# Perceiver layer: scores of two heads on the two halves of the array, keys out of PSUM in one instruction per engine

## What is computed

```
q = (layernorm(x) @ Wq + bq)   # 16 heads of 64
k = (ctx @ Wk + bk);  v = (ctx @ Wv + bv)
weights = softmax(q k^T / 8);  x = x + (weights v) @ Wo + bo
```

## Time and profile before

| | us |
|---|---|
| median of three runs | 1577.32 |
| span of the profiled execution | 1574.1 |
| TensorE matmul busy | 1500.4 (95%) |
| VectorE busy | 913.4 (58%) |
| ScalarE busy | 600.4 (38%) |

### The profile page before, as it was taken

One profiled execution on the slowest core, in us unless ns is written; L12 is line 12 of the kernel. 1 busy time (PEld: TensorE's weight loads), 2 busy tenths in 40 slices (PEclk: granted clock), 3 DMA queues, 4 the chain that ended last, 5 costly groups with the idle time before them and its releaser, 6 DMA issues. The chain is left out here.

```text
span 1574.1 us, 24321 instructions
## 1 busy us (share of the span) xinstructions
PE 1500.4 (95%) x8628; PEld 1178.7 (75%) x8628; DVE 913.4 (58%) x1868; ACT 600.4 (38%) x1238; POOL 54.4 (3%) x56
## 2 busy tenths in 40 slices
PE   6899999999999999899999999999999989799999
PEld 3587778777777787687778777777777677588777
DVE  4445753674467447734763575457535555576779
ACT  2324631653256226522641364246315524331120
POOL 3000000000000000000000000000000012200002
PEclk9999999999999999999999999999999988989999
DMA  6600100031011002300100032001003140023210
GB/s 234 201 7 28 33 22 8 28 97 52 9 35 41 8 8 62 103 18 2 54 22 7 15 95 74 8 14 41 14 1 88 27 95 27 1 85 104 82 53 27
DMA packets 87056, 75.96 MB, mean 48 GB/s; under 512 B 9120, under 2 KB 66496, under 8 KB 86928
## 3 DMA queue, kind: packets, MB, share of 16 engines
q1 hardware_dynamic: 85600, 70.29, 15.1%
q0 software_dynamic: 1328, 3.99, 0.9%
HBM read 69.01 MB, written 5.24 MB: 47 GB/s over the span
## 5 line engine op out<-in xcount | busy, mean ns | idle before, releaser
L606 PE MATMUL b_ps<-ctxT,wk 128*128 128x512 f32 x1536 | 410.9, 403 | 9.4 <-DVEq L536 4.5
L597 PE MATMUL b_ps<-wv,ctxT 128*128 128x512 f32 x1536 | 368.2, 398 | 3.6 <-DVE ctxT L195 3.6
L597 PEld LDWEIGHTS b_ps<-wv,ctxT 128*128 128x128 f32 x1536 | 286.8, 188 | 75.4 <-issue 10.9
L606 PEld LDWEIGHTS b_ps<-ctxT,wk 128*128 128x128 f32 x1536 | 281.3, 190 | 67.9 <-issue 7.5
L853 DVE TENSOR_SCALAR_CACHE_REDUCE b_prob<-b_ps 128x512 f32<-128x512 f32 x256 | 176.9, 691 | 211.1 <-PE b_ps L618 209.1
L773 ACT ACTIVATE b_kst<-b_ps,b_bkT 64x512 fp32r<-64x512 f32 x256 | 174.7, 682 | 247.4 <-PE b_ps L606 244.2
L801 DVE COPY b_V<-b_ps 128x512 f32<-128x512 f32 x128 | 88.6, 692 | 253.5 <-PE b_ps L597 253.3
L752 ACT COPY b_pT<-b_ps 128x512 f32<-128x512 f32 x128 | 75.2, 588 | 418.2 <-PE b_ps L627 417.5
L867 DVE SCALAR_TENSOR_TENSOR b_kst<-b_ps,b_bkT,b_kst 64x512 fp32r<-64x512 f32 x256 | 191.8, 749 | 18.2 <-ACT b_kst L773 7.8
L764 ACT ACTIVATE b_prob<-b_prob,b_negm 128x512 f32<-128x512 f32 x256 | 183.0, 717 | 1.9
L618 PE MATMUL b_ps<-b_kst,q 128*128 128x512 f32 x512 | 160.9, 395 | 5.3 <-DVE b_prob L853 4.4
(11 more groups left out here) (207 smaller groups left out, 1227.1 us busy)
## 6 DMA issues: line engine op xcount, KB each, us to landing
stage<-in_ctx SPq DMA_DIRECT2D x32, 512.0 KB, 3.8
q<-q_s SPq DMA_DIRECT2D x128, 64.0 KB, 2.4
stage<-in_L_xattn_Wk SPq DMA_DIRECT2D x30, 256.0 KB, 3.1
stage<-in_L_xattn_Wv SPq DMA_DIRECT2D x28, 256.0 KB, 2.8
w_tiles<-in_L_ffn_q_proj SPq DMA_DIRECT2D x16, 256.0 KB, 4.1
w_tiles<-in_L_ffn_k_proj SPq DMA_DIRECT2D x16, 256.0 KB, 3.8
w_tiles<-in_L_ffn_v_proj SPq DMA_DIRECT2D x16, 256.0 KB, 3.8
w_tiles<-in_L_ffn_o_proj SPq DMA_DIRECT2D x16, 256.0 KB, 3.3
```

What stands on the lines that cost most here:

```text
L597: mm = nc.tensor.matmul(ps[:, bank], ctxT[:, a, k, c * P:(c + 1) * P], wv[:, w, k], start=m == 0 and k == 0, stop=m == 2 and k == C - 1)
L606: mm = nc.tensor.matmul(ps[:, KB + t % 2], wk[:, i % 2, w, k], ctxT[:, a, k, s * BANK:(s + 1) * BANK], start=m == 0, stop=m == len(terms) - 1)
```

## The change

- `score` is called once per block. For each of the three terms (q hi with key hi, q lo with key hi, q hi with key lo) it issues two 64-row products, head 0 from partitions 0 to 63 and head 1 from 64 to 127, into the banks `QB` and `QB + 1`: six instructions of 64 rows where four of 128 rows were.
- P is issued whole, all 12 products, and S behind it. There is one key bank, so P of block t waits for the lo parts of block t-1 (before: t-2).
- The keys leave PSUM with one ScalarE and one VectorE instruction of 128 rows each (before: two and two of 64 rows).
- VectorE's score copies read the two banks; both wait for the last of the six products.
- `q` in SBUF is half as large and is loaded with one DMA (before: four).

```diff
-    KB, QB, TB, OB = 0, 2, 3, 5
+    KB, QB, TB, OB = 0, 1, 3, 5
 def load_q(sp, Z, X, q_s, b, i):
-    for half in range(2):
-        for h in range(2):
-            sp.dma_start(X.q[half * Z.HD:(half + 1) * Z.HD, i % 2, h].bitcast(F32),
-                         q_s[:, i, h * Z.HD:(h + 1) * Z.HD, b * P:(b + 1) * P].rearrange("l d t -> d l t")
-                         ).then_inc(X.q_in[i % 2].sem, 16)
+    sp.dma_start(X.q[:, i % 2].bitcast(F32), q_s[:, i, :, b * P:(b + 1) * P].rearrange("l d t -> d l t")
+                 ).then_inc(X.q_in[i % 2].sem, 16)
...
-            def score(b, t, h):
+            def score(b, t):
...
-                reach(pe, klo_done, b, 2 * t + h + 1)
-                reach(pe, qk_out, b, 2 * t + h)
-                for l in range(2):
-                    mm = nc.tensor.matmul(ps[:, QB], q[:, i % 2, h, l], kst[:, t % 2, h], start=l == 0, stop=l == 1)
+                reach(pe, klo_done, b, t + 1)
+                reach(pe, qk_out, b, 2 * t)
+                for m, (l, a) in enumerate(((0, 0), (1, 0), (0, 1))):
+                    for h in range(2):
+                        rows = slice(h * HD, (h + 1) * HD)
+                        mm = nc.tensor.matmul(ps[:, QB + h], q[rows, i % 2, l], kst[rows, t % 2, a], start=m == 0, stop=m == 2)
                 mm.then_inc(qk_psum.sem, 1)
...
-                    reach(pe, klo_done, batch, 2 * (n - 1))
-                    project(n, 0, 6)
+                    reach(pe, klo_done, batch, n)
+                    project(n, 0, 3 * C)
                 if exists(e, more):
-                    score(*own(b, e), 0)
-                if exists(t, more):
-                    project(n, 6, 3 * C)
-                if exists(e, more):
-                    score(*own(b, e), 1)
+                    score(*own(b, e))
...
-                    for h in range(2):
-                        rows = slice(h * HD, (h + 1) * HD)
-                        nc.scalar.activation(kst[rows, m % 2, h], ps[rows, KB + m % 2], ACT.Identity,
-                                             bias=bkT[rows, m // SB:m // SB + 1]).then_inc(khi_done.sem, 1)
+                    nc.scalar.activation(kst[:, m % 2, 0], ps[:, KB], ACT.Identity,
+                                         bias=bkT[:, m // SB:m // SB + 1]).then_inc(khi_done.sem, 1)
...
-                    for h in range(2):
-                        rows, other = slice(h * HD, (h + 1) * HD), slice((1 - h) * HD, (2 - h) * HD)
-                        reach(dve, khi_done, batch, 2 * m + h + 1)
-                        nc.vector.scalar_tensor_tensor(kst[other, m % 2, h], ps[rows, KB + m % 2],
-                                                       bkT[rows, m // SB:m // SB + 1], kst[rows, m % 2, h].bitcast(F32),
-                                                       ALU.add, ALU.subtract).then_inc(klo_done.sem, 1)
+                    reach(dve, khi_done, batch, m + 1)
+                    nc.vector.scalar_tensor_tensor(kst[:, m % 2, 1], ps[:, KB], bkT[:, m // SB:m // SB + 1],
+                                                   kst[:, m % 2, 0].bitcast(F32), ALU.add, ALU.subtract
+                                                   ).then_inc(klo_done.sem, 1)
```

More of the change, by code:

```diff
@@ L142, in __init__ @@
         self.ctxT = sb("ctxT", [P, 2, Z.C, Z.S], F32R)
-        self.q = sb("q", [P, 2, 2, 2, P], F32R)
+        self.q = sb("q", [P, 2, 2, P], F32R)
         self.wo = sb("wo", [P, Z.NP, Z.D])
@@ L150, in __init__ @@
         self.chi_done = count("chi_done", Z.NC, Z.NC)
-        self.q_in = [count(f"q_in{i}", 4 * 16 * Z.NP // 2, 0) for i in range(2)]
+        self.q_in = [count(f"q_in{i}", 16 * Z.NP // 2, 0) for i in range(2)]
         self.stage = Stage(ctx, nc, Z)
@@ L510, in cross_attention @@
         k_psum = sem("k_psum", STEPS)
-        qk_psum = sem("qk_psum", 2 * STEPS)
+        qk_psum = sem("qk_psum", STEPS)
         t_psum = sem("t_psum", NP * ROUNDS)
@@ L514, in cross_attention @@
         r_psum = sem("r_psum", NP)
-        khi_done = sem("khi_done", 2 * STEPS)
+        khi_done = sem("khi_done", STEPS)
         exp_done = sem("exp_done", 2 * STEPS)
         te_done = sem("te_done", NP * ROUNDS // 2)
-        klo_done = sem("klo_done", 2 * STEPS)
+        klo_done = sem("klo_done", STEPS)
         qk_out = sem("qk_out", 2 * STEPS)
@@ L578, in _ @@
                     if i is not None and (more or i < NP):
-                        reach(sp, qk_psum, (b, 0), 2 * SB * (i - 1))
+                        reach(sp, qk_psum, (b, 0), SB * (i - 1))
                         load_q(sp, Z, X, q_s, b + i // NP, i % NP)
@@ L605, in project @@
                     a, w, k = terms[m]
-                    mm = nc.tensor.matmul(ps[:, KB + t % 2], wk[:, i % 2, w, k], ctxT[:, a, k, s * BANK:(s + 1) * BANK],
+                    mm = nc.tensor.matmul(ps[:, KB], wk[:, i % 2, w, k], ctxT[:, a, k, s * BANK:(s + 1) * BANK],
                                           start=m == 0, stop=m == len(terms) - 1)
@@ L609, in project @@
                     mm.then_inc(k_psum.sem, 1)
-            def score(b, t, h):
+            def score(b, t):
                 i = t // SB
-                if t % SB == 0 and h == 0:
-                    reach(pe, X.q_in[i % 2], b, 64 * (i // 2 + 1))
-                reach(pe, klo_done, b, 2 * t + h + 1)
-                reach(pe, qk_out, b, 2 * t + h)
-                for l in range(2):
-                    mm = nc.tensor.matmul(ps[:, QB], q[:, i % 2, h, l], kst[:, t % 2, h], start=l == 0, stop=l == 1)
+                if t % SB == 0:
+                    reach(pe, X.q_in[i % 2], b, 16 * (i // 2 + 1))
+                reach(pe, klo_done, b, t + 1)
[4 more added lines that the diff above has]
+                        mm = nc.tensor.matmul(ps[:, QB + h], q[rows, i % 2, l], kst[rows, t % 2, a], start=m == 0, stop=m == 2)
                 mm.then_inc(qk_psum.sem, 1)
@@ L769, in step @@
                     reach(act, k_psum, batch, m + 1)
-                    reach(act, qk_psum, batch, 2 * (m - 1))
-                    for h in range(2):
-                        rows = slice(h * HD, (h + 1) * HD)
-                        nc.scalar.activation(kst[rows, m % 2, h], ps[rows, KB + m % 2], ACT.Identity,
-                                             bias=bkT[rows, m // SB:m // SB + 1]).then_inc(khi_done.sem, 1)
+                    reach(act, qk_psum, batch, m - 1)
+                    nc.scalar.activation(kst[:, m % 2, 0], ps[:, KB], ACT.Identity,
+                                         bias=bkT[:, m // SB:m // SB + 1]).then_inc(khi_done.sem, 1)
                 chunks_hi(rest)
@@ L847, in step @@
                     for h in range(2):
-                        reach(dve, qk_psum, batch, 2 * e + h + 1)
+                        reach(dve, qk_psum, batch, e + 1)
                         reach(dve, t_psum, batch, ROUNDS * (i - 2) + 2 * (s + 1))
@@ L852, in step @@
                             reach(dve, negm_done, batch, i - 1)
-                        nc.vector.tensor_scalar(prob[:, i % 2, h, s * BANK:(s + 1) * BANK], ps[:, QB], 1.0, None,
+                        nc.vector.tensor_scalar(prob[:, i % 2, h, s * BANK:(s + 1) * BANK], ps[:, QB + h], 1.0, None,
                                                 ALU.mult, ALU.max, accum_out=mx[:, i % 2, h, s:s + 1]).then_inc(qk_out.sem, 1)
```

## The result

The changed kernel takes 1600.75 us (median of 4 runs, 1597.22 to 1603.6) against 1578.03 for the kernel before in the same comparison: ratio 1.0152, 95% interval 1.0129 to 1.0175. It is 1.5% slower; the forecast was 1605, 1.7%.

What follows compares the result with a forecast made beforehand. TensorE, busy 95% of the span, was taken as the bound; waits in bare steps and at the start, less gains elsewhere, summed to +27.5 us on 1577.3: 1605 us, 1.7% slower, chance 0.70, range 1585 to 1640.

Steps and rivals of the forecast that it cites:

- the new wait: P of block t+1 waits for block t's key lo part, behind both score copies: 0.60 us in each bare step.
- bare steps: Block steps without ring items, 69 followed by another P: ordinary ones 6.32 us for 5.76, those with `mt` 6.81.
- two score copies at 0.73 each: VectorE's link in the chain between S's end and the key lo part, taking it from 3.96 to 5.42 us.
- some 52 times, some 40 us: Sign in the profile: P's first product idle until VectorE's key lo part, about 0.6 and 1.1 us each.
- Pairs overlap fully: S's three pairs of 64-row products take 3 x 0.23 = 0.69 us, not 1.39 one after the other.
- Rivals A and C: S's pairs do not overlap, 1693 us, chance 0.10 (A); they overlap only partly, 1643 us, chance 0.08 (C).
- way in: TensorE's switch from full array to row halves ahead of S: 0.19 us added, bounds 0 and 0.25.
- rival B: Way into the row halves costs nothing and the last product comes out sooner: not slower, 1578 us, chance 0.12.
- TensorE's own work: Time of TensorE's products per step, without the wait: falls by only 0.04 us, S 0.97 in place of 1.01.
- steps 33: Change of batch: one q load for four ends the context transposes' DMA wait, -2.6 us each, -7.7 in all.
- The start: P of block 1 must wait for the first key part, then one chain of 6.32: 71.5 for 67.58, +3.9 us.
- The prediction's estimate for two tiles: From the page's 3.07x for four row tiles: some 0.12 us lost per S, the sum 15 us higher.

Runs made afterwards that it cites:

- key_first: Changed kernel with VectorE's key lo part moved ahead of the two score copies, `mt` and `negm`: 1574.23 us, ratio 0.9982 to the kernel before.
- before_one_bank: Kernel before the change with only the second key bank taken away, full-array products kept: 1617.81 us, ratio 1.0255 to the kernel before.
- same_half: Changed kernel with all six products of S on rows 0 to 63 of the array (computes other scores): 1689.67 us, ratio 1.0721 to the kernel before.
- unpaired: Changed kernel with S's six products ordered head 0 three times, then head 1 three times: 1598.53 us, ratio 1.0139 to the kernel before.
- fill_start: Changed kernel with 8 unused products ahead of the key wait of each of blocks 1 and 2: 1588.28 us, ratio 1.0084 to the kernel before.
- pad16: Changed kernel with 8 tiny unused products (16 TensorE instructions) in front of the loop over batches: 1594.71 us, ratio 1.0114 to the kernel before.
- before_pad16: Kernel before the change with 8 tiny unused products (16 TensorE instructions) in front of the loop over batches: 1584.07 us, ratio 1.0045.

## Why the prediction was right

- The step that carried it, the new wait, held. P waits for the key lo part, behind both score copies; the time is 4 us from the forecast and inside 1585 to 1640. key_first and before_one_bank show the cause from both sides. That the total came so close is luck in part: the bare steps were put 13.3 us too high, and other steps 11.4 too low.
- Its size was off. I had 6.32 and 6.81, it is 6.02 and 6.63, so bare steps cost +22.1 and not +35.4. The term that was mis-sized is "two score copies at 0.73 each": back to back, 627.16 to 627.77 to 628.38, they take 0.61. The 0.73 of the earlier trace rows was the way from a copy to an instruction that starts only behind the copy's end (0.69), as `mt` does. The 64-row key part of before_one_bank does so too (603.40, behind a copy from 602.66), though it doesn't need the copy; the 128-row one of the changed kernel starts 0.08 before the copy's end. The 0.15 to a waiting product was 0.06. The sign "some 52 times, some 40 us" of idle time at P was not met either: the page shows 15.7 us, behind the 19 steps with `mt` and at the start. The waits are shorter than forecast, and the modelled ends hide those of the ordinary steps.
- Pairs overlap fully: 0.90 from S to W, for 0.88 reckoned; the first start comes 0.10 late and the second pair 0.11. Rivals A and C fall (same_half, unpaired). The round trip of the earlier trace rows was a good row for the way in, and rival B falls with it.
- TensorE's own work fell by 0.02 to 0.03 per step (5.72 to 5.75 in key_first), as good as nothing. The 0.04 counted for the steps with ring items came to 0.6 us in all others of the table, for 2.0.
- The end of the wait in steps 29 (-2.1) was exact; steps 33 gave -6.6 for -7.7.
- The start cost 6.5 and not 3.9. The chain was right, but its idle times brought the clock down to its lower level, 1.2 GHz, for parts of the next two projections (4.4 and 4.5 us in place of 3.0). I left that out. fill_start, where TensorE does not stand there, has the full clock.
- Missed altogether: +6.3 at the jumps back. By pad16 and before_pad16 it is not a work of the change itself, but of where its code begins. It made up half of what the chain fell short: without it the change would have read about 1594, 1.0% slower. The sum has no term for it.

## What to carry to other kernels

A buffer given up turns the consumer's program order into a chain: write down what the freeing instruction stands behind, and if it is not urgent work, move the freeing instruction ahead before counting the change as a loss. Here that one move, at no cost, took back all of the 22 us in bare steps. In a kernel with a hardware loop, compare the steps at the jump separately; 16 harmless instructions moved their sum up by 7 us in one kernel and down by 9.5 in the other, more than many a change is worth.

## What the runs showed of the hardware

- Two 64-row products on different row halves run at the pace of one (the second and third pair start 0.23 apart), and the halves take their products independently of the order between them: unpaired is as fast as pairs (1598.5 and 1600.8 us, S 0.97 in both). The Trainium skill, "TensorE: Matmul & The Clock Gate", Part 3, says that matmuls start and end in program order; the starts of unpaired differ from that, and the measurement decides. The prediction's estimate for two tiles from the same page's figure for four (3.07x), some 0.12 us more per S, was not borne out: S took 0.90 us to W where 0.88 was reckoned for full overlap, and 0.69 more on one half.
- The change to half arrays cost 0.10 us ahead of the first pair (it starts 0.33 behind P's last product, for 0.23 between full ones) and 0.11 ahead of the second (0.34 behind the first); with six products for four it ate the gain.
- Idle time of TensorE at a jump back of the loop: 0.85 to 1.40 us in all 28 jumps traced, and in 22 of them 0.75 to 2.99 us more a few instructions on, depending on where the loop's code begins. They end 1.59 to 1.75 and 1.25 to 1.61 us behind the end of a 16 KB packet of the instruction queue.
- VectorE starts a score copy 0.61 us behind the one before it, and `mt`, which needs the copy's result, 0.73 behind.
